# A second-attention stage whose weights and first context block are loaded by the stage before it, with its preparing work in another order

## The reference

```python
# x = x + tanh(g_xattn[1]) * L1_xattn(layernorm(x), ctx, ctx, ...)
Q = (q @ Wq.T + bq).reshape(bs, sl, H, HD)      # H = 16, HD = 32
K = (k @ Wk.T + bk).reshape(bs, sl, H, HD)
V = (v @ Wv.T + bv).reshape(bs, sl, H, HD)
score = jnp.einsum('bshd,bsgd->bshg', Q, K)
weight = jax.nn.softmax(score, axis=-1)
attn = jnp.einsum('bshg,bsgd->bshd', weight, V).reshape(bs, sl, nf)
```

## Time and profile before

| What | us |
|---|---|
| median of 3 runs | 2358.07 (2353.35 to 2362.89) |
| the profiled execution | 2350.3 |
| its span | 2348.5 |
| PE matmul busy | 2119.5 (90%) |
| POOL, DVE, ACT busy | 1207.5, 1051.3, 916.9 |

### The profile page before, as it was taken

The page is one execution under the profiler, slowest core; times in us unless marked ns, Lnnn a source line. Parts: engine busy times, 40 slices in busy tenths (PEclk is TensorE's granted clock), DMA queues, the critical chain, the costliest instruction groups (busy, mean ns, idle before and its releaser), DMA issues. The chain is left out here.

```text
span 2348.5 us, 30901 instructions
## 1 busy us (share of the span) xinstructions
PE 2119.5 (90%) x10728; PEld 1730.3 (74%) x10728; DVE 1051.3 (45%) x1582; ACT 916.9 (39%) x1709; POOL 1207.5 (51%) x861
## 2 busy tenths in 40 slices
PE   6999999999999996999899999997598875689998
PEld 5888788778878885788677777775477754468886
DVE  3556556644665475224223333333465343585110
ACT  4335334433534362212133343332267766223332
POOL 6755775477447753411666566663534322444332
PEclk9999999999999998799999999998799877799999
DMA  4222322232133313401045444444785553513000
GB/s 149 90 87 75 126 90 90 68 130 99 63 100 116 117 38 101 143 19 54 19 145 172 160 147 159 148 142 175 197 220 165 128 143 102 188 33 99 18 18 18
DMA packets 171450, 255.49 MB, mean 109 GB/s; under 512 B 45808, under 2 KB 70384, under 8 KB 169552
## 3 DMA queue, kind: packets, MB, share of 16 engines
q1 hardware_dynamic: 160048, 213.09, 29.0%
q0 software_dynamic: 8704, 25.19, 3.8%
q10 hardware_dynamic: 2592, 15.73, 1.7%
HBM read 200.45 MB, written 53.52 MB: 108 GB/s over the span
## 5 line engine op out<-in xcount | busy, mean ns | idle before, releaser
L1089 PE MATMUL b_gate_up<-b_h_hl,b_gu_hl 128*128 128x512 f32 (+1 forms) x1656 | 398.1, 399 | 3.9 <-POOL b_gu_hl L890 3.3
L238 POOL TENSOR_TENSOR a_w_hl<-a_w_raw,a_w_hl 128x2048 fp32r<-128x2048 f32 x65 | 299.9, 4614 | 163.3 <-ACT a_w_hl L300 163.2
L1089 PEld LDWEIGHTS b_gate_up<-b_h_hl,b_gu_hl 128*128 128x128 f32 (+1 forms) x1656 | 299.3, 182 | 89.5 <-POOL b_gu_hl L890 3.4
L901 POOL TENSOR_TENSOR b_a_hl<-b_prod,b_a_hl 128x512 fp32r<-128x512 f32 (+1 forms) x69 | 88.9, 1290 | 255.8 <-ACT b_a_hl L997 255.3
L1101 PE MATMUL b_y_sum<-b_dn_hl,b_a_hl 128*128 128x512 f32 (+1 forms) x828 | 199.1, 398 | 6.2 <-POOL b_a_hl L901 3.4
L413 PE MATMUL a_proj<-a_c_hl,a_w_hl 128*128 128x512 f32 x768 | 183.7, 399 | 20.1 <-DVE a_w_hl L530 18.1
L992 ACT ACTIVATE b_silu<-b_gate_up 128x512 f32<-128x512 f32 (+1 forms) x69 | 41.2, 597 | 392.2 <-PE b_gate_up L1089 375.0
L1101 PEld LDWEIGHTS b_y_sum<-b_dn_hl,b_a_hl 128*128 128x128 f32 (+1 forms) x828 | 159.0, 193 | 43.0 <-POOL b_a_hl L901 4.7
L300 ACT ACTIVATE a_w_hl<-a_w_raw 128x2048 fp32r<-128x2048 f32 x66 | 126.2, 1912 | 163.3 <-PE a_proj L413 106.7
L413 PEld LDWEIGHTS a_proj<-a_c_hl,a_w_hl 128*128 128x128 f32 x768 | 146.5, 193 | 52.6 <-issue 18.1
L487 PE MATMUL a_proj<-a_w_hl,a_a_hl 128*128 128x512 f32 x768 | 179.6, 392 | 3.9 <-DVE a_a_hl L586 3.9
(11 more groups left out here) (223 smaller groups left out, 3749.3 us busy)
## 6 DMA issues: line engine op xcount, KB each, us to landing
b_gu_raw<-in_b_gate_up SPq DMA_DIRECT2D x68, 352.0 KB
a_w_raw<-in_a_ki_w SPq DMA_DIRECT2D x18, 1024.0 KB, 5.1
a_w_raw<-in_a_vi_w SPq DMA_DIRECT2D x16, 1024.0 KB, 5.1
a_w_raw<-in_a_q_w SPq DMA_DIRECT2D x16, 1024.0 KB, 5.0
a_w_raw<-in_a_o_w SPq DMA_DIRECT2D x16, 1024.0 KB, 5.5
l_expert_out<-b_yg ACTq DMA_DIRECT2D x14, 1024.0 KB, 5.7
b_dn_raw<-in_b_down SPq DMA_DIRECT2D x34, 256.0 KB
p_w_piece<-in_w_ffn SPq DMA_DIRECT2D x32, 256.0 KB, 2.9
```

What stands on the lines that cost most here:

```text
L238: pool.tensor_tensor(w_hl[:, s, 1], w_raw[:, s], f32(w_hl[:, s, 0]), ALU.subtract)\
L901: pool.tensor_tensor(a_hl[0:w, 1, f, :], prod[0:w, (NF * par + f) % 2, :], f32(a_hl[0:w, 0, f, :]), ALU.subtract).then_inc(a_split, 1)
L1089: mm = pe.matmul(gu_ps[0:w, n, part, :], gu_hl[:, s, wp, k, cols], h_hl[:, hslot, ap, k, :], start=(k == 0 and m == 0), stop=(k == KC - 1 ...
```

## The change

The 12 weight loads and the 4 ctx loads of block 0 are issued by SP at the end of `l0_experts`, after its last store of `y`, and SP waits for them before the barrier. They land in `carry`, one buffer of 128 x 8192 that both stages use: in the experts it is `y`, in the attention it is `early` and `c_raw`. The twelve semaphores of the weight loads are gone. One is added in the expert stage.

In the opening, SP now begins with the x tiles, `bias` and `v_b`. ACT makes all v copies right behind K and ctx, and one q copy behind each K take. POOL makes the power and the next gather tile by tile, and the four q splits after the gather of tile 5. DVE takes v item j after normalising tile j; its wait for the constants stands before v item 0 and no more before tile 0.

In the loop, for blocks with one to follow, the items h 2 and h 3 come before v 2 and v 3. SP stores both of these v items in the block's step 6.

```diff
@@ -687,7 +687,7 @@
         h_hl = sb("h_hl", [P, 2, 2, KC, BLK], F32R)
-        y = sb("y", [P, NT, D])
+        y = carry.rearrange("p (n d) -> p n d", d=D)
         gu_hl = sb("gu_hl", [P, 2, 2, KC, 2 * F], F32R)
@@ -853,11 +854,17 @@
                 load_group_weights(2 * t + 2, 0)
+            sp.wait_ge(x_out, 16 * NBLK)
+            for n, (src, width) in enumerate([(W_k, D) for W_k in next_W] + [(next_ctx, BLK)]):
+                for k in range(KC):
+                    at = (n * KC + k) * D
+                    sp.dma_start(carry[:, at:at + width], src.rearrange("(k p) n -> k p n", p=P)[k][:, 0:width])\
+                        .then_inc(next_in, 16)
+            sp.wait_ge(next_in, 16 * (len(next_W) + 1) * KC)
             sp.wait_ge(yg_out, 16 * (MAXG - 1) + 16)
...
                 sp.wait_ge(rows_out[j], 16 * NBLK)
-            sp.wait_ge(x_out, 16 * NBLK)
 
@@ -1388,8 +1395,8 @@
         if n + 1 < NBLK:
-            ITEMS += [("v", n, 0), ("h", n + 1, 0), ("v", n, 1), ("h", n + 1, 1), ("v", n, 2), ("h", n + 1, 2),
-                      ("h", n + 1, 3), ("v", n, 3)]
+            ITEMS += [("v", n, 0), ("h", n + 1, 0), ("v", n, 1), ("h", n + 1, 1), ("h", n + 1, 2), ("h", n + 1, 3),
+                      ("v", n, 2), ("v", n, 3)]
             ITEMS += [("q", n + 1, j) for j in range(4)]
@@ -1422,8 +1429,6 @@
         w_hl = sb("w_hl", [P, 3, 2, KC, D], F32R)
-        early = sb("early", [P, 3 * KC * D])
-        c_raw = sb("c_raw", [P, KC, BLK])
         c_hl = sb("c_hl", [P, 2, KC, BLK], F32R)
@@ -1451,14 +1456,15 @@
 
-        w_raw = early[:].rearrange("p (n k d) -> p n k d", n=3, k=KC)
+        early = carry[:, 0:3 * KC * D]
+        c_raw = carry[:, 3 * KC * D:3 * KC * D + KC * BLK].rearrange("p (k n) -> p k n", n=BLK)
+        w_raw = early.rearrange("p (n k d) -> p n k d", n=3, k=KC)
         q_sb = early[:, 0:H * TQ].rearrange("p (h t) -> p h t", h=H)
...
         masked = sem("masked")
-        w_in = [[sem(f"w_in{n}_{k}") for k in range(KC)] for n in range(3)]
         w_high = [sem(f"w_high{n}") for n in range(3)]
@@ -1615,17 +1616,10 @@
 
-            for k in range(KC):
-                load_w("k", k)
-                load_ctx(0, k)
-            for k in range(KC):
-                load_w("v", k)
             for j in range(TPB):
...
             sp.dma_start(v_b[:], W["bv"].to_broadcast([P, D])).then_inc(const_in, 16)
-            for k in range(KC):
-                load_w("q", k)
             for j in range(TPB):
@@ -1661,9 +1655,12 @@
                     if w >= 3 and n + 1 < NBLK:
-                        if w < 7:
+                        if w in (3, 4):
                             store("v", n, w - 3)
-                        else:
+                        elif w == 6:
+                            store("v", n, 2)
+                            store("v", n, 3)
+                        elif w == 7:
                             load_v(n)
@@ -1739,17 +1736,11 @@
                 w_low("v", k)
-            for n in range(3):
+            for n in range(TPB):
                 power(n)
-                if n < 2:
-                    gather(n + 2)
-            for k in range(2):
+                gather(n + 2)
+            for k in range(KC):
                 w_low("q", k)
-            power(3)
-            for k in range(2, KC):
-                w_low("q", k)
-            gather(4)
-            gather(5)
             for n in range(TPB, 2 * TPB):
@@ -1774,12 +1765,11 @@
                     act.wait_ge(item_ready, last("v", b - 1))
-                act.wait_ge(c_in[k], 16 * (b + 1))
+                    act.wait_ge(c_in[k], 16 * b)
                 act.activation(by_turn(c_hl[:, 0, k, :]), by_group(c_raw[:, k, :]), ACT.Copy).then_inc(c_high, 1)
...
                 n = WHICH[name]
-                act.wait_ge(w_in[n][k], 16)
                 act.activation(w_hl[:, n, 0, k, :], w_raw[:, n, k, :], ACT.Copy).then_inc(w_high[n], 1)
@@ -1848,14 +1838,11 @@
                 c_high_part(0, k)
+            for k in range(KC):
+                w_high_part("v", k)
             act.wait_ge(const_in, 32)
-            for k in range(2):
+            for k in range(KC):
                 take("k", 0, k)
-                w_high_part("v", 2 * k)
-                w_high_part("v", 2 * k + 1)
-            for k in range(2, KC):
-                take("k", 0, k)
-            for k in range(KC):
                 w_high_part("q", k)
@@ -2083,18 +2070,18 @@
                 c_low(0, k)
-            dve.wait_ge(const_in, 32)
             tile_stats(0)
...
             tile_normalise(0)
+            dve.wait_ge(const_in, 32)
+            take_v(0, 0)
             tile_stats(2)
             tile_normalise(1)
-            take_v(0, 0)
+            take_v(0, 1)
             tile_stats(3)
             tile_normalise(2)
-            take_v(0, 1)
+            take_v(0, 2)
             tile_normalise(3)
-            take_v(0, 2)
             take_v(0, 3)
```

19 lines of the change are left out of this document (9 added, 10 removed).

## The result

| | before | after |
|---|---|---|
| median of 5 runs, us | 2356.22 (2353.35 to 2362.89) | 2343.29 (2336.89 to 2345.97) |
| the profiled execution, us | 2350.3 | 2345.97 |
| its span, us | 2348.5 | 2344.2 |

The ratio is 0.9932 (95% interval 0.9915 to 0.9949), by which the change gives 16.0 us (12.0 to 20.0); the medians differ by 12.9. The forecast was 2341.8, 1.5 us from the measured median. The largest term behind it did less well: the opening was to give 12.3 us and gave about two thirds of that. The profiled execution of the changed kernel is the slowest of its five and that of before lies 5.9 us under its median, so the two profiles differ by 4.3 us only.

A forecast was written before the change was run, and what follows sets the result against it. The attention opening was taken as a chain of waits with no engine full. Terms 11.3 + 1.0 + 4.0 = 16.3 us off the profiled 2350.3 gave 2334.0, or 2341.8 for a median; range 2333 to 2354.

The forecast's parts named there:

- The early loads: End of expert stage: 16 loads take under 28 us of SP's 40.9 us wait, hidden with 13 us to spare.
- Gain 0: Start of attention opening: DVE's start hangs on POOL, not weights, so K items 0 and 1 stay put; gain 0.
- its end past 1615: Sign that would overturn the sum: the expert stage grows and ends later than 1615 us.
- The bias row: Opening: v_b, issued 6th instead of 18th, lands by 1629.4 before anyone asks; ACT takes K item 0 at 1630.9.
- DVE's order: Opening: DVE takes v item 0 before tile 2; tile 3 starts at 1646.6 instead of 1657.88, 11.3 us earlier.
- tile 3 waiting for its gather past 1649: Opening, sign of being wrong: DVE's tile 3 still held by its gather after 1649 us, against about 1647 expected.
- the ctx loads that ran beside the slow one now start 2 us after the gather, not with it: Opening: reason for pricing tile 3's gather at 3.9 us after its last issue started, landing at 1644.0 rather than 1649.6.
- Rival (C): Opening and loop: tile 3's gather lands late, x loads give nothing, loop gain cancelled; 8.3 us, 2349.8; chance 0.31.
- From tile 3 to q: Opening: SP's chain keeps its length, the 11.3 us come through, gathers leaving the x loads add 1.0 (bounds 0 and 3.3).
- rule of turns between queues: Opening: each DMA engine serves queues packet by packet, so all 3.3 us would return and the forecast be 2.3 us lower.
- The loop: Steps 4 to 6, blocks 1 and 2: reordered h and v items let q start sooner; 2.0 us each, 4.0 together.
- Rival (D): Loop step 5: both v items at half speed, ACT never catches up; 8.0 us lost per block, 2362.8; chance 0.06.

The follow-up runs named there:

- late_loads: Changed kernel with the 16 loads made by SP after the barrier again, bias and v_b ahead of them, all new orders kept; 0.9960 of before.
- vb_early: Kernel before with only the loads of bias and v_b put first in SP's queue; 1.0003 of before.
- x_first: Changed kernel with SP's four x loads of token block 1 ahead of the K loads and v stores of block 0; 0.9943 of before.
- dve_splits_v: Changed kernel with the four v weight splits moved from POOL to DVE; 0.9963 of before.
- all_three: Changed kernel with v splits on DVE, block 1's x loads first, and block 0's h splits ahead of tiles 4 to 7; 0.9890 of before.
- the opening alone: Changed kernel with the old order of items and stores in the loop; 0.9964 of before.
- the loop alone: Kernel before with only the loop's new order of h and v items and new stores of v 2 and 3; 0.9982 of before.
- after_timed: Changed kernel, unchanged, timed again on the chip of the other experiments; 0.9942 of before.

## Why the prediction was right in the total and wrong in its largest term

**The early loads** were hidden as worked out (33.3 us of SP's wait are left, the trace begins them at 1582). "Gain 0" was true of DVE's start, 5.69 us into the stage as before (5.61), behind POOL's iota. It was wrong of what follows: with the new orders, late weights and late x cost about 2 us of the first q item, most of it through the weights (late_loads). The sign "its end past 1615" did appear in the first profile, where the attention stage began 6.8 us late; two more executions of the same kernel began at 1617.3 and 1617.4, so it was spread.

**The bias row** was right in its signs (no wait for `v_b`, K items from 1632 in one piece) and wrong as the cause. The step "so ACT takes K item 0 at 1630.9, and PE runs on" needs more than `v_b`. vb_early has that wait gone, and gains at most 1.4 us. Tile 3 owes it 3.0 us of its 8.2.

**DVE's order** is the term that was mis-sized. Tile 3 was to come 28.7 us into the stage, 11.3 earlier; it came at 31.8, 8.2 earlier (30.6 to 31.8 in four executions), and one sign of being wrong, "tile 3 waiting for its gather past 1649", came true (1649.7 on the clock of before). The 3.1 us are three pieces of the step. v item 0 was ready 0.7 us later than 24.3, since the fifteen matmuls that end K items 0 and 1 ran at 0.82 of the clock and took 4.44 us, not 3.68. Tile 2 then waited 1.33 us for its gather, and tile 3 waited 1.08 us for its own.

The gathers were mis-priced more than they were issued late. From the start of the last issue to DVE they had been given 3.9 us and took 6.0 and 7.8; the issue of tile 3's ended 25.0 us into the stage against an estimate of 23.5. The premise was that "the ctx loads that ran beside the slow one now start 2 us after the gather, not with it". They started with it:

```profile
1648.52 2.26 SPq L1558 DMA_DIRECT2D carry<-in_ctxT  x4
1648.76 0.96 POOL L1703 DMA_INDIRECT p_routed<-l_expert_out,place  x1 [0.31 <-issue]
```

In x_first they really come later, 5.0 us after the gather's last issue, and the gather is quick. The view of tile 3's gather (median us from issue to landing) in after, from 1647 to 1650, then in x_first, from 1644.5 to 1648:

```profile
carry<-in_ctxT SPq DMA_DIRECT2D x3, 256.0 KB, 5.1
l_kT<-p_outs SPq DMA_DIRECT2D x1, 256.0 KB
p_routed<-l_expert_out,place POOLq DMA_INDIRECT x2, 6.7
```

```profile
l_kT<-p_outs SPq DMA_DIRECT2D x2, 256.0 KB, 3.0
p_routed<-l_expert_out,place POOLq DMA_INDIRECT x2, 4.4
```

Over all traces, a gather of tile 2 or 3 took 6.9 to 9.3 us from the start of its last issue (to DVE where DVE waited for it, else to its landing) where the ctx loads were issued before it or within 0.4 us after it (fourteen gathers). It took 5.4 to 6.0 where they came 1.0 to 3.4 us later (seven), and 4.2 in x_first. The one that gave the price, 3.9 with the loads 1.9 us behind it, is the quickest of all, so even the premise would have asked for more. Rival (C), with 8.3 us for this link and "a gather that finds any ctx load beside it is slow", had both the size and, as far as this goes, the reason. No run moved the ctx loads alone, and why tile 2's gathers took 5.4 to 6.0 with the new orders stays open.

POOL's splits had a smaller part. They were priced at 6.2 us and took 7.10, and tile 0's power came 0.3 us after its estimate. The row that gave the price was mixed: two of its three splits, 1.74 and 1.73 us, stood beside adds of VectorE, the third, 1.29, did not. In before, DVE beside these splits, and then two splits alone:

```profile
1638.57 0.94 DVE L2012 SCALAR_TENSOR_TENSOR p_xr<-p_routed,weight,p_xr 128x512 f32<-128x512 f32 x1
...
1639.54 1.66 DVE L2015 SCALAR_TENSOR_TENSOR p_xr<-p_routed,weight,p_xr 128x512 f32<-128x512 f32 x1
```

```profile
1653.03 2.50 POOL L1723 TENSOR_TENSOR p_w_hl<-p_early,p_w_hl 128x512 fp32r<-128x512 f32 x2
```

In after three adds of 1.67 to 1.72 us stand beside them. With the splits gone from POOL the gather's issue ends at 23.8, near the estimate, and tile 3 comes at 29.2 in dve_splits_v but at 30.8 in all_three.

**From tile 3 to q** the forecast gave 1.0 us more, and the trace took 1.4 (35.1 us against 33.7). The step that failed is "gathers 4 and 5 ran beside these loads and now precede them": only gather 4 does. Gather 5 waits for power 3, and so for DVE, and is issued at 1661.5, half a microsecond before x. The DMA view of 1656 to 1671 still has the gathers' queue beside the others, as in the earlier trace rows:

```profile
q0 software_dynamic: 320, 1.05, 25.6%
...
p_xr<-x_shared SPq DMA_DIRECT2D x3, 256.0 KB, 6.4
```

The prediction's rule of turns between queues, by which 3.3 us would have come back, could not be put to the test, since the transfers it was to free never moved apart.

So first q comes at 65.7 to 67.0 in four executions, 7.3 us earlier than the 73.7 and 74.0 with the old opening, and the time of the opening alone gives 8.5 (5.4 to 11.3). The forecast of 12.3 is outside that. The signs say the same: x of tile 4 came 7.1 us earlier and not 11, and the first scores at 98.1 us (1716 on the clock of before), not at 1708.

**The loop** was forecast at 4.0 us, with 3.5 per block as the end of its range. The time of the loop alone gives 4.2 (1.6 to 7.0). The last v item ends 2.2 us later than before in its block, by the mask of step 4 (12.5 against 10.3 us; 2.6 forecast), q runs at full speed, and 3.3 and 2.9 us per block are kept in the traces: "because ACT started 2.6 us late and has to catch up" was too careful. Its lateness holds up nothing. Rival (D) needed v items of 4 us or more and found 3.07 and 2.98; by the rule that it cites it needed a gap before them, and that gap was 0.73 us.

The sum of 16.3 itself is not refuted: it was 12.9 by the medians of the first chip, 16.0 (12.0 to 20.0) by their ratio and 13.7 (8.7 to 18.8) by that of after_timed. What the halves test is the terms: they measure 8.5 us for the 12.3 of the opening and 4.2 for the 4.0 of the loop. Against the medians the sum is 3.4 us too large, and 1.9 of these are covered because the median of before over five runs is 2356.2 and not the 2358.1 of the three that the forecast started from; that part is luck. The total is right with one term about a third too large and one perhaps a third too small, and its chief cause, the bias row, gives little by itself.

## What to carry to other kernels

Before you price a wait that goes, list every input of the instruction behind it and when each is ready: here a row, a tile of x, a copy on another engine and a gather were due within 8 us of each other, and taking one away gave next to nothing. Price a gather by one with the same traffic beside it, and move that traffic on your time line together with the gather. Price work on GpSimd by rows with as many VectorE instructions of two SBUF operands beside it, and keep long runs of it away from them. And where PE stands for long, ask first in which order the engine it waits for does its work: moving four instructions of 0.7 us ahead of four tiles brought the first scores forward by some 11 us in the profiles, this whole change by 4 to 8.
